# A graph network's attention layer: the self loops taken out of the gathered edge lists

## The reference

```python
_loop = jnp.arange(3125)
src, dst = concatenate([_s, _d, _loop]), concatenate([_d, _s, _loop])   # then sorted by dst
...
Q, K, V = (hn @ Wq), (hn @ Wk), (hn @ Wv)              # (n, 8 heads, 16)
score = clip(einsum('ehd,ehd->eh', K[src], Q[dst]) / sqrt(HD), -5, 5)
a = exp(score - segment_max(score, dst)[dst])
a = a / segment_sum(a, dst)[dst]
wV = segment_sum(V[src] * a[:, :, None], dst)
h2 = h + wV @ Wo + bo                                  # then batch norm, two dense layers, residual
```

## Time and profile before

| | us |
|---|---|
| median of 3 runs (lowest, highest) | 1321.13 (1319.81, 1322.50) |
| the profiled execution | 1321.58 |
| its span, first to last instruction | 1319.8 |
| first to last gather's start | 654.45 to 1175.67 |
| first instruction after the attention | 1190.17 |

### The profile page before, as it was taken

The page is one execution under the profiler, slowest core; times in us unless marked ns, Lnnn a source line. Parts: engine busy times, 40 slices in busy tenths (PEclk is TensorE's granted clock), DMA queues, the critical chain, the costliest instruction groups (busy, mean ns, idle before and its releaser), DMA issues. The chain is left out here.

```text
span 1319.8 us, 18063 instructions
## 1 busy us (share of the span) xinstructions
PE 986.8 (75%) x6084; PEld 628.7 (48%) x6084; DVE 859.4 (65%) x2017; ACT 519.9 (39%) x1055; POOL 412.9 (31%) x514
## 2 busy tenths in 40 slices
PE   1288898989999999794666666666665666647997
PEld 1176777545555556353533444444443443424654
DVE  3887888423543466566467788887888878775343
ACT  1155555201211111111465666655666555533210
POOL 4000000000000000000277777777777777750000
PEclk9998988989999999897855667676677666657999
DMA  6020000700000000000453333333333333327111
GB/s 154 24 51 1 1 1 1 237 10 0 5 5 0 17 16 19 17 1 21 127 147 104 106 104 106 106 104 104 105 107 104 104 107 105 105 75 168 48 46 30
DMA packets 51077, 89.00 MB, mean 67 GB/s; under 512 B 13714, under 2 KB 36389, under 8 KB 50610
## 3 DMA queue, kind: packets, MB, share of 16 engines
q0 software_dynamic: 20608, 55.20, 14.5%
q1 hardware_dynamic: 27888, 31.05, 8.6%
q10 hardware_dynamic: 2492, 1.61, 0.5%
HBM read 71.83 MB, written 15.99 MB: 67 GB/s over the span
## 5 line engine op out<-in xcount | busy, mean ns | idle before, releaser
L1630 POOL DMA_INDIRECT counts_all<-kv_d,counts_all x416 | 395.7, 951 | 146.3 <-issue 139.0
L812 PE MATMUL bank<-counts_all,parts 125*128 125x500 f16 (+2 forms) x1400 | 274.9, 355 | 21.4 <-DVE parts L1077 9.7
L812 PEld LDWEIGHTS bank<-counts_all,parts 125*128 125x128 f16 x1400 | 127.6, 98 | 158.0 <-issue 13.5
L1506 POOL IOTA iota_n<- 128x256 f16 x1 | 0.3, 342 | 596.4 <-issue 596.4
L1810 PE MATMUL bank<-counts_all 125*128 125x128 f16 x1230 | 135.2, 290 | 52.7 <-ACT counts_all L1912 52.2
L1810 PEld LDWEIGHTS bank<-counts_all 125*128 125x128 f16 x1230 | 111.0, 134 | 97.5 <-ACT counts_all L1912 97.0
L1825 PE MATMUL bank<-counts_all,parts 128*128 128x272 f16 x615 | 135.4, 378 | 8.7 <-DVE counts_all L1678 6.9
L1721 DVE TENSOR_TENSOR counts_all<-counts_all,bank 128x512 f32<-128x512 f32 x104 | 71.5, 687 | 105.0 <-DMA counts_all<-kv_d,counts_all 104.8
L978 ACT CAST counts_all<-bank 125x500 f16<-125x500 f32 (+1 forms) x157 | 91.7, 594 | 85.0 <-PE bank L756 85.0
L1799 PE MATMUL bank<-rel_rows,ident_h 104*128 104x512 f16 x104 | 57.3, 551 | 79.3 <-ACT away L1902 58.8
L1902 ACT ACTIVATE away<-bank,lane_bias 125x512 f16<-125x512 f32 x173 | 110.8, 680 | 1.1 <-PE bank L1799 0.7
(11 more groups left out here) (288 smaller groups left out, 1430.4 us busy)
## 6 DMA issues: line engine op xcount, KB each, us to landing
counts_d<-counts_all SPq DMA_DIRECT2D x1, 6835.9 KB
counts_all<-kv_d,counts_all POOLq DMA_INDIRECT x416
counts_all<-counts_d SPq DMA_DIRECT2D x1, 4785.2 KB
kv_d<-counts_all SPq DMA_DIRECT2D x6, 448.0 KB
counts_all<-counts_d SPq DMA_DIRECT2D x3, 683.6 KB
inv_deg<-invdeg_d SPq DMA_DIRECT2D x1, 1562.5 KB, 6.9
q_d<-counts_all SPq DMA_DIRECT2D x1, 1562.5 KB
x<-in_x SPq DMA_DIRECT2D x6, 250.0 KB
```

What stands on the lines that cost most here:

```text
L812: last = T.matmul(agg_ps[p][:, 0:w], pin[:, s, part, :], counts[:, s, bass.ds(b * BLK, w)], start=(s + part == 0), stop=(s + part == NT))
L1630: G.indirect_dma_start(out=out_rows, out_offset=None, in_=table_d, in_offset=bass.IndirectOffsetOnAxis(ap=index, axis=0)).then_inc(signal, 16)
```

## The change

The 3125 self loops leave the gathered lists. What remains, 50,000 edges, makes 391 chunks; 25 chunks more, one a tile, hold the loops of the tile's nodes. Such a chunk stands in the middle of its tile's edges, so there are again 416 chunks in 104 groups, and 25 groups have a loop chunk. It needs no gather: SyncE copies 128 consecutive rows of `kv_d` (`own_rows`), and VectorE waits for that copy too.

The lists without loops are made by GpSimd in the five layers' block. It waits for `built`, loads windows of `dst` and `src` into the buffer `early_buf` (six loads, twice), finds the loops, shifts the other entries up in seven steps of 1 to 64 places, and counts faults: 256 instructions with a semaphore each, nearly all of which the next one waits for. TensorE waits for the 256th before layer 4, transposes the lists (8 products), ScalarE copies them back, and GpSimd makes the relative node numbers and the verdict (some 140 smaller instructions) before the block's end. The tables of limits that the set-up made for this, and the store and load of `reldst`, are removed. The attention's branch now reads the new verdict, on SyncE too.

```diff
+E2 = E - N
+CHE = -(-E2 // LANES)
...
+LOOPS_BEFORE = {round((t + 0.5) * E2 / NT / LANES): t for t in range(NT)}
+for e_ in range(CHE):
+    if e_ in LOOPS_BEFORE:
+        EDGES_OF.append(None)
+        LOOPS_OF.append(LOOPS_BEFORE[e_])
+    EDGES_OF.append(e_)
+    LOOPS_OF.append(None)
+CTILES = [[LOOPS_OF[c]] if EDGES_OF[c] is None else ETILES[EDGES_OF[c]] for c in range(CH)]
...
-                    for t_ in range(NT):
-                        of = [g for g in range(NG) if GTILES[g][0] == t_]
-                        if of:
-                            last = G.memset(glim[:, of[0]:of[-1] + 1], float(t_ * TILE))
...
-                    st.done(V.tensor_tensor(under[:, :], dstN[:, 0:CH], clim[:, 0, :], ALU.subtract))
-                    st.done(V.tensor_tensor(over[:, :], dstN[:, 0:CH], clim[:, 1, :], ALU.subtract))
...
+step = Steps(pool, list_step)
+pool.wait_ge(built, 1)
+step.run(G.memset(faults, 0.0))
+for half in range(2):
+    a, b_, c_, d_ = [v[:, :, 0:SPAN] for v in (p0, p1, p2, p3)]
...
+                    pool.dma_start(into.bitcast(i32)[r0 - first:r1 - first, g, 0:SPAN + 1],
+                                   bass.AP(tensor=listed.tensor, offset=136 * r0 - MARGIN,
+                                           ap=[[136, r1 - r0], [1, SPAN + 1]])).then_inc(list_load, 16)
...
+    pool.wait_ge(list_load, 16 * 6 * (half + 1))
...
+    step.run(G.tensor_tensor(d_, d_, c_, ALU.mult))
+    add_faults(d_)
...
+    for bit in range(6, -1, -1):
+        step.run(G.tensor_scalar(to, d_, float(2 ** bit), float(2 ** (6 - bit)), ALU.is_ge, ALU.mult))
+        if bit < 6:
+            step.run(G.tensor_tensor(a, a, c_, ALU.add))
+        if bit:
+            step.run(G.tensor_scalar(c_, d_, float(2 ** bit), float(2 ** bit), ALU.is_ge, ALU.mult))
+            step.run(G.tensor_tensor(d_, d_, c_, ALU.subtract))
+    for bit in range(7):
+        k, top = 2 ** bit, float(2 ** (6 - bit))
+        step.run(G.tensor_scalar(c_, a, top, None, ALU.is_ge))
+        step.run(G.tensor_tensor(d_, c_, b_, ALU.mult))
+        step.run(G.tensor_tensor(b_, b_, d_, ALU.subtract))
+        step.run(G.tensor_tensor(b_[:, :, 0:SPAN - k], b_[:, :, 0:SPAN - k], d_[:, :, k:SPAN], ALU.add))
+...
+assert step.n == ROWS_STEPS, step.n
+pool.wait_ge(by_lane_ready, 2)
...
+for t_, c0, c1 in spans_of([ts[0] for ts in ETILES]):
+    step.done(G.tensor_scalar(low[:, c0:c1], dst_by_lane[:, c0:c1], float(t_ * TILE), None, ALU.is_lt))
...
+step.run(G.partition_all_reduce(worst, faults, 128, bass.bass_isa.ReduceOp.absmax))
...
                     @block.tensor
+if KINDS[l] == "message":
+    pe.wait_ge(list_step, ROWS_STEPS)
+    for bank, halves in ((6, (0, 3)), (7, (2, 1))):
+        for g in range(CROWG):
+            last = T.transpose(ps[bank][:, g * CROWS:(g + 1) * CROWS], pairs(halves[g // 2])[:, g % 2, 0:LANES],
+                               ident[0:CROWS, 0:CROWS])
+        last.then_inc(lists_turned, 1)
...
                     @block.scalar
+    act.wait_ge(lists_turned, 2)
+    S.copy(dst_by_lane, ps[6][:, 0:CROWS * CROWG]).then_inc(by_lane_ready, 1)
+    S.copy(src_by_lane, ps[7][:, 0:CROWS * CROWG]).then_inc(by_lane_ready, 1)
...
-            reldst = carve([LANES, CHP])
+            reldst = att_rel
-                return load_registers(nc, engine, flags[0:1, 0:4], NT)[1]
+                return load_registers(nc, engine, att_flags[0:1, 0:4], NT)[1]
...
                 @block.sync
+                    wide = windows_spanned(ET.SP)
+                    def own_rows(g):
+                        for k in range(GRP):
+                            tile = LOOPS_OF[g * GRP + k]
+                            if tile is not None:
+                                if g >= RING:
+                                    sp.wait_ge(va_ready, g - RING + 1)
+                                r0 = min(tile * TILE, N - LANES)
+                                sp.dma_start(kv[:, g % RING, k, :], kv_d[r0:r0 + LANES, :]).then_inc(loops_in, 16)
+                    with sp.If(wide <= 1):
+                        for g in range(RING):
+                            own_rows(g)
                     sp.dma_start(q_d.rearrange("(t p) c -> p t c", p=TILE), Q[:, :, :, :].rearrange("p t h c -> p t (h c)")
...
+                    with sp.If(wide <= 1):
+                        for g in range(RING, NG):
+                            own_rows(g)
...
                 @block.gpsimd
-                                c = g * GRP + k
-                                gather(kv[:, g % RING, k, :], kv_d, srcidx[:, c:c + 1], kv_in[g % RING])
+                                e = EDGES_OF[g * GRP + k]
+                                if e is not None:
+                                    gather(kv[:, g % RING, k, :], kv_d, att_src[:, e:e + 1], kv_in[g % RING])
...
                 @block.vector
+                            if g in groups_with_loops:
+                                dve.wait_ge(loops_in, 16 * (groups_with_loops.index(g) + 1))
```

More of the change, by code:

```diff
@@ L74, with spans_of @@
 LAST_OF = [c // GRP for c in LAST_CHUNK]
+def spans_of(values):
+    spans, at = [], 0
+    for value, same in groupby(values):
+        n = len(list(same))
+        spans.append((value, at, at + n))
+        at += n
+    return spans
 SPILL = 15
@@ new lines, in _ @@
+                        assert step.n == ROWS_STEPS, step.n
+                        step.done(G.iota(loop_lane, pattern=[[0, 1]], base=0, channel_multiplier=1, allow_small_or_imprecise_dtypes=True))
+                        step.run(G.memset(att_flags, 0))
+                        step.run(G.tensor_scalar(lane_after, loop_lane, float(TILE), NO_NODE, ALU.is_ge, ALU.mult))
+                        short = LANES - TILE
+                        step.done(G.tensor_scalar(lane_term, loop_lane, float(short), NO_NODE, ALU.is_lt, ALU.mult))
@@ new lines, in _ @@
+                        step.wait()
+                        step.run(G.tensor_tensor(low, low, high, ALU.add))
+                        n_ = CHE - 1
+                        step.run(G.tensor_tensor(low[:, 0:1], low[:, 0:1], low[:, n_:n_ + 1], ALU.add))
+                        n_ //= 2
+                        step.run(G.tensor_tensor(low[:, 0:n_], low[:, 0:n_], low[:, n_:2 * n_], ALU.add))
+                        for k in range(1, 5):
+                            step.run(G.tensor_tensor(low[:, 0:39], low[:, 0:39], low[:, 39 * k:39 * (k + 1)], ALU.add))
@@ new lines, in _ @@
+                        step.run(G.tensor_copy(att_flags[:, 1:2], worst[:, 0:1]))
+                        for c in range(CH):
+                            t0_ = GTILES[c // GRP][0]
+                            if EDGES_OF[c] is None:
+                                t_ = LOOPS_OF[c]
+                                lane = loop_lane_end if t_ == NT - 1 else loop_lane
+                                step.done(G.tensor_scalar(att_rel[:, c:c + 1], lane, float((t_ - t0_) * TILE), None, ALU.add))
+                        for (t0_, shift), c0, c1 in spans_of([(GTILES[c // GRP][0], None if EDGES_OF[c] is None else c - EDGES_OF[c])
+                                                              for c in range(CH)]):
+                            if shift is not None:
+                                step.done(G.tensor_scalar(att_rel[:, c0:c1], dst_by_lane[:, c0 - shift:c1 - shift],
+                                                          -float(t0_ * TILE), None, ALU.add))
@@ L1444, in build @@
             kv_in = [sem(f"kv_in{i}") for i in range(RING)]
+            loops_in = sem("loops_in")
+            groups_with_loops = [c // GRP for c in range(CH) if LOOPS_OF[c] is not None]
+            assert all(h - g >= RING for g, h in zip(groups_with_loops, groups_with_loops[1:]))
             pool_waits = sem("pool_waits")
```

165 lines of the change are left out of this document (129 added, 36 removed).

## The result

The changed kernel takes 1328.48 us (median of 8 runs, 1326.03 to 1329.52) against 1321.06 us before (8 runs): a ratio of 1.0049, 95% interval 1.0035 to 1.0064. It is slower by 0.5%, not faster by 1.5%. The profiled span grew by 6.4 us, from 1319.8 to 1326.2. The attention gave back 25.6 us, and the five layers lost 31.5.

The account below looks back on a forecast made before the run. Gather issue on GpSimd was taken to bound the attention, TensorE the layers. Against the profiled execution: 1321.58 - 31.4 + 6 + 4 + 1 = 1301.2 us, said as 1301; likeliest range 1294 to 1307, 8 in 10 1289 to 1319.

Parts of the forecast that it names:

- The bound of the attention: Attention: the issue of GpSimd's gathers paces it, 5.02 us a group against VectorE's mean of 3.95 us.
- 25 x 1.255 = 31.4 us: Attention: 25 of 416 gathers go, each saving a full interval of 1.255 us, all of it counted as gain.
- the chain's price: Five layers: GpSimd's 256 list instructions take 201 us, so the chain, begun at 266, ends near 505 us.
- 27 us of standing still for VectorE: Layers 1 and 2: GpSimd stands still for three VectorE operations a block, 0.69 us each, over 13 blocks.
- the list, 0 in the sum: Before layer 4: the list is ready with 29 us to spare, so TensorE's wait for it costs 0.
- the bounds of 99 to 319 us: Five layers: least and greatest length of GpSimd's list chain, from the cost of fills and memsets.
- My charge of about 0.5 us for each meeting: Layers 1 to 3: a VectorE operation needing the shared access waits 0 to 1.07 us for GpSimd; layer ends cost 6 us.
- the 2.5 us a block: Layer 3: VectorE may wait at five places a block, 2.5 us, of which 1.5 us is covered by reserve.
- 10.2 for 4: Layer 3: VectorE falls 1 us behind a block for four to five blocks, charged 4 us, between 0 and 27.
- Rival 3: Before layer 4: the list comes late and TensorE waits for the 256th instruction; halfway 1340 us, up to 1391; chance 0.13.
- deadline of 534 us: Before layer 4: the list may come up to 534 us at no cost, inside TensorE's gap before that layer.
- Rivals 2: Layer 3: VectorE falls behind, waiting a whole GpSimd instruction at five places a block; 1307 to 1332 us, around 1314; chance 0.14.

## Why the prediction was wrong

**The bound of the attention** was read rightly: gathers pace it, no other engine took over but for one gap of 1.47 us, the copies cost nothing. The term "25 x 1.255 = 31.4 us" was 5.8 too large. A gather's interval is not a constant: it grows where the gather begins while VectorE's low part still has over 0.23 us to run. Before, 7 gathers behind the first did; now 19 do. That the loop chunks shift the phase between the two engines is my reading, not shown; neither the list work nor the copies are needed for it, as 24 gathers are long without the list work and 24 without both. I had held the lock up against VectorE alone and not against the gathers.

**The failed step** is the chain's price: "I take 1.05 ns for one input and for fills, twice that for two inputs, and 0.2 us fixed: 115 + 35 + 51 = 201 us." For two inputs it nearly held: 149 us by my figures, 153 measured, and some 13 of gaps of 0.08 us between instructions. For one input it was out by a factor of more than two: 47 us by my figures, 108 measured and 6 of gaps. With VectorE mostly out of the way, in the run with `u` in PSUM, the two are 148 and 100. I had taken fills for the nearest rows and put arithmetic on one input beside them; it costs 1.26 us at 416 elements with one operation and 1.6 with two, more than with two inputs. With the start 12.8 us late (the store 4.9, the gap 6.9, two casts) and, in place of 27 us of standing still for VectorE, 12.8 (288.0 - 275.2), the chain ended at 566.8, not at 505. So the list, 0 in the sum, cost 15.6 us of waiting at layer 4. The chain lay inside the bounds of 99 to 319 us; the middle was wrong.

**VectorE.** Two inputs in SBUF count: such operations went from 692 to 1026 ns. The rule of the Trainium skill ("SBUF — State Buffer", section "SBUF: two separate sides") has it so. Normalizations with one input in SBUF were held too, 342 against 676; whether they ran in a double-rate mode, the rule's other kind, no run here shows. My charge of about 0.5 us for each meeting was near at the layers' starts (4.8 for 6). In layer 3 the 2.5 us a block came out by luck (17.2 us in seven blocks): half of it is the 25 normalizations of `u`, 1.2 us a block, which I had counted as one place, and the other operations cost 0.1 to 0.6 us each. Layer 3 was undercharged, 10.2 for 4, mainly since GpSimd worked through the whole of it and not for four to five blocks: a consequence of the chain.

**Rival 3** named the mechanism that turned the sign, at 0.13. Its deadline of 534 us moved, though, since VectorE made layer 3 end later; the list cost 15.6 us and not the 33 of 566.8 - 534. Rivals 2 and 3 came together, which no case of mine priced. The second part's 140 instructions were free, as I had said: layer 4 behind the transposes runs as before (568.20 to 654.75, 86.6 us; before, 536.26 to 623.22, 87.0).

A version that beats both kernels came out of this: 1289.5 to 1290.1 us. Some 9 of its 31 us are the moved store, which the kernel before can have too.

## What to carry to other kernels

Before work goes to an idle engine, price its instructions by form from a row of that form, and where there is none, let the forecast follow the upper bound: a chain whose end somebody waits for turns an error of some 0.27 us an instruction (69 us over 256, without VectorE's share) into tens of microseconds. VectorE and GpSimd are not independent while both work from SBUF: keep one operand of VectorE's operations in PSUM where the two run side by side, and count the meeting in both directions. Put the consumer of a background chain as late as its own successors allow, and keep large stores out of the way of small loads that start a chain.

## What was not expected of the hardware

- GpSimd, 98 x 416 float32, with VectorE mostly out of the way (the runs with `u` in PSUM): two inputs 1.07 us; one input and one operation 1.26; one input with a compare or a maximum and a second operation 1.61.
- Its first two-input operation came 6.93 us late; an earlier dummy took that away. The Trainium skill ("GPSIMD Engine Reference", section "Instruction dispatch") gives some 6 us for the first call of freshly loaded code; that loading is the cause here is not shown. In the changed kernel the partition reduce and the first operation behind it waited 5.98 and 7.19 us again.
- VectorE with an operand in PSUM ran at 686 and 688 ns beside GpSimd, at about 1000 from SBUF.
- A gather that starts while VectorE's low part (all operands in SBUF) still has 0.27 to 0.67 us to run ends 0.81 to 0.84 us after it, in 56 of 56 cases in two runs; with less than 0.14 us to run it takes its 0.95 us.
- A store of 7.6 MB just ahead of layer 1 kept TensorE waiting 8.63 us there; begun in the middle of that layer it cost nothing visible.
